# Bias row sums of the third product's stage: GpSimd's in place multiplications and additions in place of the vector engine's fused ones

## What is computed

```python
x = x + L0_ffn(L0_cond(x))       # L0_ffn: xf @ W_base.T + b_base + routed low-rank part
x = x + L1_ffn(L1_cond(x))       # L1_cond: x @ weight.T + bias + scale * delta
# L1_ffn: x @ base_W.T + routed low-rank part, routed by x @ router_W.T
```

## Times and profile before

| | us |
|---|---|
| runs (3) | 901.51, 902.22, 912.92 |
| median | 902.22 |
| the profiled execution, whole | 901.23 |
| its span (first to last instruction) | 899.5 |
| TensorE busy | 893.7 (99%) |
| VectorE busy | 673.8 (75%) |
| ScalarE busy | 326.7 (36%) |
| GpSimd busy | 147.3 (16%) |

### The profile page before, as it was taken

One profiled execution on the slowest core, in us unless ns is written; L12 is line 12 of the kernel. 1 busy time (PEld: TensorE's weight loads), 2 busy tenths in 40 slices (PEclk: granted clock), 3 DMA queues, 4 the chain that ended last, 5 costly groups with the idle time before them and its releaser, 6 DMA issues.

```text
span 899.5 us, 13649 instructions
## 1 busy us (share of the span) xinstructions
PE 893.7 (99%) x4646; PEld 782.0 (87%) x4646; DVE 673.8 (75%) x1473; ACT 326.7 (36%) x545; POOL 147.3 (16%) x298
## 2 busy tenths in 40 slices
PE   9999999999999999999999999999999999999998
PEld 8999998888998888888888888888888888888887
DVE  6899899866587968888676677767766767767764
ACT  6578778411334423233322222222222222222220
POOL 0100010111002001414212312302302202302300
PEclk9999999999999999999999999999999999999999
DMA  9523330765412042575786887887887887886885
GB/s 360 194 83 114 121 126 25 255 217 170 143 51 95 0 141 100 186 264 199 230 300 245 295 296 256 285 293 251 287 304 247 288 292 257 284 300 243 293 276 195
DMA packets 60979, 192.52 MB, mean 214 GB/s; under 512 B 7761, under 2 KB 10730, under 8 KB 58990
## 3 DMA queue, kind: packets, MB, share of 16 engines
q1 hardware_dynamic: 50188, 160.04, 49.5%
q0 software_dynamic: 10432, 31.35, 11.8%
q10 hardware_dynamic: 290, 0.26, 0.1%
HBM read 159.39 MB, written 32.76 MB: 214 GB/s over the span
## 4 chain that ended last, share of the span: by engine, by line
PE 96%; DMA 3%; DVE 1%; ACT 0%; SPq 0%; issue 0%; DVEq 0%
PE bank L900 29%; PE bank L554 15%; PE bank L555 15%; PE bank L556 15%; PE bank L882 6%; PE bank L868 4%; PE bank L877 2%; PE bank L701 2%; DMA t_lo<-t_scratch 2%; PE bank L991 2%; DMA m_raw<-m1t 1%; PE bank L811 1%; PE bank L615 1%; PE bank L828 0%; PE bank L826 0%; PE bank L574 0%
## 5 line engine op out<-in xcount | busy, mean ns | idle before, releaser
L900 PE MATMUL bank<-g_hi,xs 128*128 128x512 f32 x448 | 152.6, 398 | 0.0
L525 POOL DMA_DIRECT2D p1sel<-p_scratch x128 | 65.6, 512 | 339.8 <-issue 339.7
L900 PE MATMUL bank<-t_hi,xs 128*128 128x512 f32 x328 | 109.2, 393 | 0.6 <-DMA t_lo<-t_scratch 0.6
L900 PEld LDWEIGHTS bank<-g_hi,xs 128*128 128x128 f32 x448 | 83.2, 188 | 15.7
L900 PE MATMUL bank<-g_lo,xs 128*128 128x512 f32 x224 | 88.4, 394 | 0.0
L1422 DVE TENSOR_TENSOR xs<-x_raw,xs 128x1024 fp32r<-128x1024 f32 x60 | 72.4, 1230 | 11.9 <-ACT xs L1068 11.9
L554 PE MATMUL bank<-gx,xs 128*128 128x304 f32 x256 | 78.3, 306 | 0.0
L556 PE MATMUL bank<-gx,xs 128*128 128x304 f32 x256 | 77.5, 303 | 0.0
L555 PE MATMUL bank<-gx,xs 128*128 128x304 f32 x256 | 77.4, 302 | 0.0
L900 PEld LDWEIGHTS bank<-t_hi,xs 128*128 128x128 f32 x328 | 61.6, 188 | 15.0 <-DMA t_lo<-t_scratch 2.0
L1068 ACT ACTIVATE xs<-x_raw 128x1024 fp32r<-128x1024 f32 x60 | 61.8, 1054 | 33.9 <-PE bank L900 33.2
(11 more groups left out here) (398 smaller groups left out, 2135.9 us busy)
## 6 DMA issues: line engine op xcount, KB each, us to landing
t_hi<-t_scratch SPq DMA_DIRECT2D x82, 512.0 KB, 5.4
t_lo<-t_scratch SPq DMA_DIRECT2D x82, 512.0 KB, 6.5
x_raw<-xq SPq DMA_DIRECT2D x16, 1024.0 KB, 6.9
out<-ost SPq DMA_DIRECT2D x62, 256.0 KB, 6.0
p1sel<-p_scratch POOLq DMA_DIRECT2D x64, 192.0 KB, 4.5
w_raw<-wall SPq DMA_DIRECT2D x16, 512.0 KB, 4.5
w<-e_scratch SPq DMA_DIRECT2D x6, 1024.0 KB, 5.1
ea<-e_scratch POOLq DMA_DIRECT2D x8, 644.0 KB, 4.4
```

What stands on the lines that cost most here:

```text
L525: pool.dma_start(f(p1sel[b][STK * s:STK * s + STK, cs]), p1_dram[bass.ds(i * STK, STK), cs]).then_inc(sems[b], 16)
L900: mm = nc.tensor.matmul(bk[j][:], l[:, c, :], m[:, c, :], start=first and c + k == 0, stop=c + k == KH + 1, skip_group_check=True)
```

## The change

GpSimd clears `bacc` and does all the arithmetic of `bias(k)`, between the loads that it issues. It has no fused instruction here: `ma` is multiplied in place by the bias column (`tensor_scalar`, 1160 columns), and is then added to `bacc` in two pieces (`tensor_tensor`, 1024 and 136 columns); `ea` is multiplied in place (1288 columns) and added (1288). The additions wait for their multiplication on a semaphore, `bias_mul`, which is `ld_wa` (at 16 from an early load) counted on. GpSimd waits for its own `ma_ok` and `mb_ok` ahead of the next load. VectorE's memset and `bias` are gone; the consumers of `mb_ok` are unchanged.

```diff
+        bias_mul = ld_wa
@@ block.gpsimd
-            for k in range(1, KC):
-                pool.wait_ge(ma_ok, k)
-                pool.dma_start(ma[:], m1t[k * P:(k + 1) * P, :]).then_inc(ld_ma, 16)
-                pool.wait_ge(mb_ok, k)
-                pool.dma_start(ea[:], e_dram[k * P:(k + 1) * P, :]).then_inc(ld_ea, 16)
+            nc.gpsimd.memset(bacc[:], 0.0).then_inc(bacc0, 1)
+            for k in range(KC):
+                pool.wait_ge(ld_ma, 16 * k + 16)
+                if k:
+                    pool.wait_ge(mb_ok, k)
+                else:
+                    pool.wait_ge(bacc0, 1)
+                nc.gpsimd.tensor_scalar(ma[:], ma[:], b1c[:, k:k + 1], None, ALU.mult).then_inc(bias_mul, 1)
+                pool.wait_ge(bias_mul, 16 + 2 * k + 1)
+                nc.gpsimd.tensor_tensor(bacc[:, 0:D], bacc[:, 0:D], ma[:, 0:D], ALU.add)
+                nc.gpsimd.tensor_tensor(bacc[:, MID0:NE], bacc[:, MID0:NE], ma[:, D:NM1], ALU.add).then_inc(ma_ok, 1)
+                pool.wait_ge(ma_ok, k + 1)
+                if k + 1 < KC:
+                    pool.dma_start(ma[:], m1t[(k + 1) * P:(k + 2) * P, :]).then_inc(ld_ma, 16)
+                pool.wait_ge(ld_ea, 16 * k + 16)
+                nc.gpsimd.tensor_scalar(ea[:], ea[:], b0c[:, k:k + 1], None, ALU.mult).then_inc(bias_mul, 1)
+                pool.wait_ge(bias_mul, 16 + 2 * k + 2)
+                nc.gpsimd.tensor_tensor(bacc[:], bacc[:], ea[:], ALU.add).then_inc(mb_ok, 1)
+                pool.wait_ge(mb_ok, k + 1)
+                if k + 1 < KC:
+                    pool.dma_start(ea[:], e_dram[(k + 1) * P:(k + 2) * P, :]).then_inc(ld_ea, 16)
@@ block.vector
-            nc.vector.memset(bacc[:], 0.0).then_inc(bacc0, 1)
-            def bias(k):
-                v.wait_ge(ld_ma, 16 * k + 16)
-                ...
-                b = b1c[:, k:k + 1]
-                nc.vector.scalar_tensor_tensor(bacc[:, 0:D], ma[:, 0:D], b, bacc[:, 0:D], ALU.mult, ALU.add)
-                nc.vector.scalar_tensor_tensor(bacc[:, MID0:NE], ma[:, D:NM1], b, bacc[:, MID0:NE],
-                                               ALU.mult, ALU.add).then_inc(ma_ok, 1)
-                v.wait_ge(ld_ea, 16 * k + 16)
-                v.wait_ge(ma_ok, k + 1)
-                nc.vector.scalar_tensor_tensor(bacc[:], ea[:], b0c[:, k:k + 1], bacc[:],
-                                               ALU.mult, ALU.add).then_inc(mb_ok, 1)
             for j in range(KC):
                 c0_out(j)
                 if j in W_AFTER:
                     w_split(W_AFTER[j])
-                for _ in range((0, 0, 1, 2, 1, 2, 2, 0)[j]):
-                    bias(done)
-                    done += 1
```

More of the change, by code:

```diff
@@ L1614, in c0_out @@
                     lo_of(c0_lo[:, j, halves[h]], c_bank(j, h)[:], c0_hi[:, j, halves[h]]).then_inc(c_lo, 1)
-            def bias(k):
-                v.wait_ge(ld_ma, 16 * k + 16)
[L1618 to L1621, removed]
-                b = b1c[:, k:k + 1]
-                nc.vector.scalar_tensor_tensor(bacc[:, 0:D], ma[:, 0:D], b, bacc[:, 0:D], ALU.mult, ALU.add)
-                nc.vector.scalar_tensor_tensor(bacc[:, MID0:NE], ma[:, D:NM1], b, bacc[:, MID0:NE],
-                                               ALU.mult, ALU.add).then_inc(ma_ok, 1)
-                v.wait_ge(ld_ea, 16 * k + 16)
-                v.wait_ge(ma_ok, k + 1)
-                nc.vector.scalar_tensor_tensor(bacc[:], ea[:], b0c[:, k:k + 1], bacc[:],
-                                               ALU.mult, ALU.add).then_inc(mb_ok, 1)
-            done = 0
             for j in range(KC):
```

## The result

| | before | changed |
|---|---|---|
| median of the runs, us | 906.1 (901.51 to 912.92, 4 runs) | 973.02 (972.35 to 973.85, 4 runs) |
| span of the profiled execution, us | 899.5 | 972.1 |
| TensorE busy, us | 893.7 | 904.6 |
| VectorE busy, us | 673.8 | 653.1 |
| GpSimd busy, us | 147.3 | 254.1 |

The ratio is 1.0787, with a 95% interval of 1.0755 to 1.0819; it goes by the fast runs, and the median of 906.1 also holds two slower ones of the kernel before (909.97 and 912.92). The direction and the place are those forecast; the size is not: +72.6 us of span were measured where +28.2 were forecast, and the time lies far above the range.

What follows compares the result with a forecast made beforehand. TensorE was taken to bound the kernel, waiting at i = 4 for the bias sums: 25.3 us of wait plus 2.9 of clock, 28.2 on 902.2, gave 930.4 us, 3.1% slower; 8 in 10 between 914 and 948.

Steps and rivals of the forecast that it cites:

- What bounds the kernel, and where it would wait: TensorE bounds; it waits at i = 4 of the h products if the bias sums end after 226.0 us; +25.3 us.
- The load of `en_raw`: SyncE's load behind `mb_ok`, wanted when i = 7 of the h products ends; still hidden, by 4 us.
- VectorE's relief worth nothing: 25.5 us of bias work and a 1.13 us memset leave VectorE; gain 0, as TensorE has no gap there.
- Start of the sums: GpSimd's first multiplication starts at 167.5 us, after its last store's issue at 166.3 and the memset of 1.13.
- The additions: On GpSimd, 2.2 ns a column: 2.43 us for 1024 columns, 0.48 for 136, 3.01 for 1288.
- The multiplications: On GpSimd, at a copy's 0.88 ns a column, upper end 1.76: 1.20 us for `ma`, 1.31 for `ea`.
- Contention: GpSimd shut out by five two-input VectorE instructions, x0's low part and four `w_lo`: 3.0 us, between 0 and 6.2.
- Cover of the loads: `ma` and `ea` loads hide behind GpSimd's arithmetic; with quicker additions they would set about 7 us a chunk.
- The clock: TensorE's standstill at i = 4 brings back 1.2 GHz for 18 matmuls: 2.9 us, lower end 0.
- The sum: Whole kernel: 25.3 us of TensorE's wait and 2.9 of clock make 28.2 us, so 930.4 us.
- The rival with multiplications at 1.76 ns: GpSimd's multiplications take 2.15 us more a chunk, 17.2 in all: 947.6 us; chance 0.20.

## Why the prediction was wrong, point by point

**What bounds the kernel, and where it would wait: right.** TensorE at i = 4, released through `b0t_hi`, `b0t_lo` and `h_add`, 2.8 us behind `mb_ok` for 2.7. One hole, none before 228 us, everything behind it later. The load of `en_raw` stayed hidden: `en_lo` ended at 293.98 + 2.43 = 296.4 us, and the product that reads it began at 309.07.

**VectorE's relief worth nothing: right**, and shown by the run without arithmetic, 1.0004.

**Start of the sums: right.** 167.77 for 167.5; the memset took 1.19 for 1.13.

**The additions: right.** 2.34, 0.47 and 2.89 us for 2.43, 0.48 and 3.01. Here the trace agrees with the estimate from the Trainium skill's GPSIMD Engine Reference, section Performance versus the Vector engine, of 2.2 ns a column.

**The multiplications: this is the step that failed.** "One stream: a copy of 288 columns takes 0.42 us undisturbed [...] I take that for the multiplication." The terms 1.20 and 1.31 measured 3.23 and 3.55 us. That is 4.27 us a chunk, 34.2 of the 36.3 us by which the sums ended later than forecast (287.6 for 251.3). A copy was the only row of one stream, but it moves values and computes nothing; even the upper end, 1.76 ns, lay below the 2.6 measured. The rows had one TENSOR_SCALAR, 0.44 us for 64 columns, and it was set aside because it also converts to integers and does two operations. It should have widened the bound all the same: 0.44 - 0.18 over 64 columns is 4 ns, and 2.6 lies between that and the copy's 0.88. What the Trainium skill's GPSIMD Engine Reference says in its section Engine selection, that one-input work is near line rate, does not hold here for a product with a factor; the measurement decides: 2.6 ns against 0.9 for the copy.

**Contention: right in kind, a little larger.** In the first three chunks GpSimd's instructions are longer by 1.0, 0.96, 1.0, 1.0 and 0.67 us than their undisturbed kind (4.23 for 3.23 and so on): 4.6 for the 3.0 taken, inside the 0 to 6.2. They are five, as forecast, each beside one of the five VectorE instructions that were named. VectorE's third and fourth `w_lo` took 2.27 and 4.16 us instead of 1.22 (the fourth beside a multiplication, of which the prediction had spoken only as an addition), and that cost nothing in the changed kernel, as TensorE's one wait shows.

**Cover of the loads: right.** No instruction of the changed kernel waits for `ma` or `ea`. With the multiplications out it is gone at times, as the 0.64 us in that run's last line shows, with 7.6 us a chunk where "about 7" was named.

**The clock: right that it falls, wrong in size.** The "up to 18 x 0.162" = 2.9 us came from the kernel's start, where 18 matmuls of 388 columns follow one another. Behind the wait come the h products, of 272 and 136 columns, and in 19 us of them the clock did not rise. It cost 10.7 us, not 2.9: 23.9 us from the release to `en_hi` with `c_hi`, and 13.1 with TensorE kept busy. What was mis-sized is how long the low clock lasts: some 6 us with the 16 wide matmuls behind the wait, over 23 with the h products.

**The sum** with the measured terms: 61.4 of standing, 10.7 of clock and 0.5 that is not placed are 72.6 us, instead of 25.3 + 2.9. The rival with multiplications at 1.76 ns had the right mechanism and a chance of 0.20, and stopped at 947.6. No rival let both terms be large together.

## What to carry to other kernels

A rate belongs to an operation and not to the number of its operands: where the trace has no row of the very operation on that engine, a copy is at best a lower bound and no estimate. Work that is moved to an idle engine must be priced against the moment at which its result is wanted; here 1.4 us of slack met a chain of eight times 14.5 us instead of eight times 6.1 (217.00 to 223.09 in the earlier trace rows). And a wait of TensorE has a second price, the clock behind it, which differed here with the instructions that followed.

## What the runs showed of the hardware that was not expected

- On GpSimd, `tensor_scalar` with one factor takes 3.23 us for 1160 float32 columns, and the same product as `tensor_tensor` with the factor's column repeated 2.13; two tiles, sum or product, take 1.40 us for 576 columns, a repeated column 1.15, a copy 0.66.
- After TensorE had stood still for 9.5 us its granted clock was 0.50 for all of the following 19 us of h products; the loss behind a wait of 61.4 us was hardly larger (10.3 and 10.7 us). With sixteen matmuls of 512 columns in front the clock was back at 1.00 in 6.2 us, and the kernel became 4.7 us shorter by them.
- A VectorE instruction with two SBUF inputs of 1024 columns took up to 4.16 us instead of 1.22 beside GpSimd's arithmetic, and GpSimd's took up to 1.0 us longer beside it.
